# Attention output produced transposed: v as a 32-column stationary operand, sums from a tile of ones, inverted as exp(-ln)

## What is computed

```python
h = jnp.maximum(_layernorm(x, axis=-1), 0.0)
...
qkv = (x @ w_qkv).reshape(b, n, 3, H, hd).transpose(2, 0, 3, 1, 4)
q, k, v = (qkv[0], qkv[1], qkv[2])
attn = jnp.einsum('bhnd,bhmd->bhnm', q, k) * scale
attn = jnp.where(attn_mask[None, None] == 0, -jnp.inf, attn)
attn = jax.nn.softmax(attn, axis=-1)
o = jnp.einsum('bhnm,bhmd->bhnd', attn, v).transpose(0, 2, 1, 3).reshape(b, n, d)
o = o @ w_proj + b_proj
mu = jnp.mean(o, axis=-1, keepdims=True)
var = jnp.mean(jnp.square(o - mu), axis=-1, keepdims=True)
ln = (o - mu) * jax.lax.rsqrt(var + LN_EPS) * ln_gamma + ln_beta
return o + ln
```

## Time and profile before

| what | value |
|---|---|
| median of 3 runs | 1971.55 us (1969.12 to 1973.96) |
| span of the profiled execution, first to last instruction | 1971.0 us |
| busy: PE / PEld / DVE / ACT / POOL | 1831.1 / 1602.2 / 1609.3 / 1084.3 / 674.6 us |
| mean granted TensorE clock, share of the full one | 0.977 |

### The profile page before, as it was taken

The page is one execution under the profiler, slowest core; times in us unless marked ns, Lnnn a source line. Parts: engine busy times, 40 slices in busy tenths (PEclk is TensorE's granted clock), DMA queues, the critical chain, the costliest instruction groups (busy, mean ns, idle before and its releaser), DMA issues.

```text
span 1971.0 us, 39957 instructions
## 1 busy us (share of the span) xinstructions
PE 1831.1 (93%) x13064; PEld 1602.2 (81%) x13064; DVE 1609.3 (82%) x4485; ACT 1084.3 (55%) x2756; POOL 674.6 (34%) x1045
## 2 busy tenths in 40 slices
PE   6899999999999999999999999999999999999974
PEld 5788888878878888888878878788888878878864
DVE  3688897888888887887888888888887988978874
ACT  3555565655655555655655655655655655655632
POOL 3233333333333333333333333333332333333331
PEclk8999999999999999999999999999999999999987
DMA  2000000000000000000000000000000000000000
GB/s 88 12 17 17 23 23 11 21 16 16 21 17 16 22 16 17 21 16 16 22 16 16 21 17 16 22 16 16 22 16 16 22 16 16 21 16 17 12 6 17
DMA packets 37975, 37.85 MB, mean 19 GB/s; under 512 B 2416, under 2 KB 37488, under 8 KB 37872
## 3 DMA queue, kind: packets, MB, share of 16 engines
q1 hardware_dynamic: 37872, 36.84, 5.7%
HBM read 20.05 MB, written 16.78 MB: 19 GB/s over the span
## 4 chain that ended last, share of the span: by engine, by line
PE 48%; DVE 25%; issue 15%; POOL 9%; ACT 3%; DVEq 0%; POOLq 0%; DMA 0%; ACTq 0%
PE bank L314 15%; PE mid L387 11%; DVE stats L683 6%; DVE x L764 5%; PE bank L322 4%; POOL o_res L909 4%; POOL rstd L899 4%; PE bank L507 3%; PE mid L370 3%; PE bank L512 3%; PE bank L487 3%; DVE x L849 3%; DVE h_t_lo L699 2%; DVE o_gam L756 2%; ACT h_t_hi L559 2%
## 5 line engine op out<-in xcount | busy, mean ns | idle before, releaser
L567 ACT ACTIVATE probs<-mid,neg_max 128x128 f32<-128x128 f32 x1024 | 284.8, 379 | 105.2 <-DVE neg_max L713 105.2
L379 PE MATMUL mid<-k_diag,q_t 128*128 128x512 f32 x512 | 273.6, 617 | 0.0
L559 ACT ACTIVATE h_t_hi<-bank 128x512 fp32r<-128x512 f32 x192 | 114.9, 599 | 251.7 <-PE bank L322 251.6
L387 PEld LDWEIGHTS mid<-v,probs_t 128*128 128x128 f32 x2048 | 244.3, 192 | 3.3
L387 PE MATMUL mid<-v,probs_t 128*128 128x33 f32 x2048 | 239.9, 272 | 0.0
L899 POOL TENSOR_TENSOR rstd<-var_eps,minus_half 128x2 f32<-128x2 f32 x320 | 226.4, 707 | 25.1
L693 DVE TENSOR_SCALAR z<-x,mean_var,rstd 128x256 f32<-128x256 f32 x384 | 205.2, 575 | 10.8 <-POOL rstd L899 3.2
L713 DVE TENSOR_REDUCE neg_max<-mid 128x8 f32<-128x1024 f32 x128 | 154.6, 1208 | 51.1 <-issue 38.0
L897 POOL TENSOR_TENSOR var_eps<-mean_var,eps 128x2 f32<-128x2 f32 x320 | 66.0, 206 | 363.9 <-DVE mean_var L687 363.9
L322 PEld LDWEIGHTS bank<-ident,z 128*128 128x128 f32 x768 | 94.8, 152 | 112.4 <-DVE z L693 73.1
L322 PE MATMUL bank<-ident,z 128*128 128x128 f32 x768 | 125.8, 288 | 61.3 <-DVE z L693 61.3
(11 more groups left out here) (133 smaller groups left out, 5485.0 us busy)
## 6 DMA issues: line engine op xcount, KB each, us to landing
x<-in_x SPq DMA_DIRECT2D x64, 256.0 KB, 2.6
out_x<-x SPq DMA_DIRECT2D x64, 256.0 KB, 2.2
w_qkv_sb<-in_w_qkv SPq DMA_DIRECT2D x1, 768.0 KB, 4.8
w_q_sb<-in_w_q SPq DMA_DIRECT2D x1, 256.0 KB, 5.0
w_k_sb<-in_w_k SPq DMA_DIRECT2D x1, 256.0 KB, 5.3
w_proj_sb<-in_w_proj SPq DMA_DIRECT2D x1, 256.0 KB, 5.2
w_v_sb<-in_w_v_t SPq DMA_DIRECT2D x1, 256.0 KB, 5.4
w_gat_sb<-in_w_gat SPq DMA_DIRECT2D x1, 256.0 KB, 5.7
```

The source lines that it names most:

```text
L379: last = pe.matmul(mid[:, s], q_t[:, par, hc, b * N:(b + 1) * N], k_diag[:, hc, :, b * N:(b + 1) * N], start=False, stop=True)
L387: last = pe.matmul(mid[:, b, h * W33:(h + 1) * W33], probs_t[:, b * HC + h // RG, h % RG], v0[:, par, b, h], start=True, stop=True)
L559: act.activation(h_t[k][0][:], bank[:], ACT.Relu).then_inc(h_hi_ready[k], 1)
L567: last = act.activation(probs[:, s, r], mid[:, s, r * N:(r + 1) * N], ACT.Exp, bias=neg_max[:, s, r:r + 1])
```

## The change

The two operands of heads times values change places. `v0` of one head, 32 columns wide, is now the stationary operand, and `probs_t` moves, 128 columns. The result has 32 partitions (features) and 128 columns (nodes), so four heads are put beneath each other with `tile_position`, which places a 32-column operand at a column of the array and its result on the partitions of the same number. The outputs of both graphs fill bank 2 of `mid` and are transposed already. The sums come from a second product in the same form, with a 128x32 tile of ones as the stationary operand; they fill bank 0, repeated over the 32 partitions of their head. ACT takes the logarithm of the sums and then exp(-x) of that. DVE multiplies the two in one instruction (`o_norm`), ACT copies `o_norm` to `o_t_hi`, and DVE subtracts. The two calls of `divide_heads` and the four transposes of `o_heads` are gone. ACT's table set is named at the start; the built program loads a table once, as before.

The wait of the first block on `probs_t` moves from the second copy to the third, since bank 2 is written from the first block on, and `scores(0)` of the next step waits for the logarithm instead of `divide_heads`. `v0` loses its 33rd column.

```diff
@@ -93,7 +92,7 @@
         ident = sb("ident", [128, 128])
         ident_b = sb("ident_b", [128, 128], bf16)
         mask_b = sb("mask_b", [128, N], bf16)
-        ones = sb("ones", [128, 1])
+        ones = sb("ones", [128, HD])
         minus_half = sb("minus_half", [128, 2])
         eps = sb("eps", [128, 2])
         turn = sb("turn", [1, 1])
...
@@ -121,13 +120,14 @@
         q_t = sb("q_t", [128, 2, HC, 2 * N])
 
         k_diag = sb("k_diag", [128, HC, RG, 2 * N])
-        v0 = sb("v0", [128, 2, 2, H, W33])
+        v0 = sb("v0", [128, 2, 2, H, HD])
         BC = 2 * HC
         neg_max = sb("neg_max", [128, BC, RG])
         probs = sb("probs", [128, BC, RG, N])
         probs_t = sb("probs_t", [128, BC, RG, N])
-        inv_sum = sb("inv_sum", [128, 2, H])
-        o_heads = sb("o_heads", [128, 2, D])
+        ln_sum = sb("ln_sum", [128, 512])
+        inv_sum = sb("inv_sum", [128, 512])
+        o_norm = sb("o_norm", [128, 512])
         o_t = parts("o_t", [128, 2, C, N])
         o = sb("o", [128, 2, D])
         o_res = sb("o_res", [128, 2, D])
...
@@ -382,17 +382,25 @@
 
                 def heads_times_values(b):
 
-                    pe.wait_ge(probs_t_ready, done(p2, BC) - HC * (1 - b))
-                    for h in range(H):
-                        last = pe.matmul(mid[:, b, h * W33:(h + 1) * W33], probs_t[:, b * HC + h // RG, h % RG],
-                                         v0[:, par, b, h], start=True, stop=True)
-                    last.then_inc(heads_psum, 1)
+                    pe.wait_ge(probs_t_ready, done(p2, BC) - (1 - b))
+                    for s in (b * HC, b * HC + 1):
+                        to = slice(s * N, (s + 1) * N)
+                        for r in range(RG):
+                            at = slice(r * HD, (r + 1) * HD)
+                            pe.matmul(mid[at, 2, to], v0[:, par, b, (s - b * HC) * RG + r], probs_t[:, s, r],
+                                      start=True, stop=True, tile_position=(0, r * HD))
+                        for r in range(RG):
+                            at = slice(r * HD, (r + 1) * HD)
+                            last = pe.matmul(mid[at, 0, to], ones[:], probs_t[:, s, r],
+                                             start=True, stop=True, tile_position=(0, r * HD))
+                    if b == 1:
+                        last.then_inc(heads_psum, 1)
 
                 if middle:
                     pe.wait_ge(q_ready, done(p2))
                     pe.wait_ge(k_ready[0], done(p2))
                     pe.wait_ge(k_ready[1], done(p2))
-                    wait_before(pe, o_heads_ready, p2, 2)
+                    wait_before(pe, ln_sum_ready, p2)
                     scores(0)
                 if front:
                     pe.wait_ge(h_hi_ready[0], done(p1))
...
@@ -415,7 +423,7 @@
                     pe.wait_ge(q_ready, done(p1))
                     rows(bank6, h_t[0], w_qkv_p, 2 * D, v0_psum)
                 if middle:
-                    wait_before(pe, o_lo_ready, p2)
+                    wait_before(pe, o_norm_ready, p2)
                     wait_before(pe, o_ready, p2)
                     scores(1)
                 if gat:
...
@@ -526,19 +534,13 @@
                     elif on_before[0]:
                         wait_before(pe, h_lo_ready[0], p0)
                     transposes(bank7, z[0], 0)
-                if middle:
-                    for b in range(2):
-                        pe.wait_ge(o_heads_ready, done(p2, 2) - (1 - b))
-                        for c in range(C):
-                            last = pe.transpose(mid[:, 2, (b * C + c) * N:(b * C + c + 1) * N],
-                                                o_heads[:, b, c * 128:(c + 1) * 128], ident[:])
-                    last.then_inc(o_t_psum, 1)
 
             run(pe, step, {0: fold, 1: masks_and_fills, 2: other_weights})
 
 
         @block.scalar
         def _(act):
+            act.preload_act_table_set("natural_log_exp_and_others")
             act.wait_ge(w_qkv_in, 16)
             act.activation(w_qkv_p[0][:], w_qkv_sb[:], ACT.Copy).then_inc(w_hi_ready, 1)
 
...
@@ -570,7 +572,7 @@
 
                 def copy_probs_t(s):
                     act.wait_ge(probs_t_psum, done(p2, BC) - (BC - 1 - s))
-                    wait_before(act, heads_psum, p2, 2)
+                    wait_before(act, heads_psum, p2)
                     act.activation(probs_t[:, s], mid[:, s], ACT.Copy).then_inc(probs_t_ready, 1)
 
                 if front:
...
@@ -645,11 +647,19 @@
                     act.wait_ge(u_psum, done(p4))
                     wait_before(act, x2_exp_ready, p4)
                     act.activation(u_exp[:].rearrange("p b d -> p (b d)"), bank4[:], ACT.Exp).then_inc(u_exp_ready, 1)
+                if middle:
+                    act.wait_ge(heads_psum, done(p2))
+                    act.activation(ln_sum[:], mid[:, 0], ACT.Ln).then_inc(ln_sum_ready, 1)
+                    act.wait_ge(ln_sum_ready, done(p2))
+                    wait_before(act, o_norm_ready, p2)
+                    act.activation(inv_sum[:], ln_sum[:], ACT.Exp, scale=-1.0).then_inc(inv_sum_ready, 1)
                 if entry:
                     relu_hi(0, p0, bank7, [k_psum])
                 if middle:
-                    act.wait_ge(o_t_psum, done(p2))
-                    act.activation(o_t[0][:], mid[:, 2], ACT.Copy).then_inc(o_hi_ready, 1)
+                    act.wait_ge(o_norm_ready, done(p2))
+                    wait_before(act, o_psum, p2)
+                    act.activation(o_t[0][:].rearrange("p b c n -> p (b c n)"), o_norm[:], ACT.Copy)\
+                       .then_inc(o_hi_ready, 1)
 
             run(act, step, {1: copy_fold})
 
...
@@ -719,17 +729,6 @@
                         dve.tensor_tensor_reduce(out=s_prod[:, b, j], in0=hw[:, b], in1=a_gat_bc[:, j],
                                                  scale=1.0, scalar=0.0, op0=ALU.mult, op1=ALU.add,
                                                  accum_out=s_sb[:, b, j:j + 1]).then_inc(s_ready, 1)
-
-                def divide_heads(b):
-
-                    heads = mid[:, b, 0:H * W33].rearrange("p (h d) -> p h d", h=H)
-                    dve.wait_ge(heads_psum, done(p2, 2) - (1 - b))
-                    dve.reciprocal(inv_sum[:, b], heads[:, :, HD]).then_inc(inv_sum_ready, 1)
-                    dve.wait_ge(inv_sum_ready, done(p2, 2) - (1 - b))
-                    wait_before(dve, o_t_psum, p2)
-                    dve.tensor_tensor(o_heads[:, b].rearrange("p (h d) -> p h d", h=H), heads[:, :, 0:HD],
-                                      inv_sum[:, b].unsqueeze(2).to_broadcast([128, H, HD]), ALU.mult)\
-                       .then_inc(o_heads_ready, 1)
 
                 if middle:
                     maxima(0)
...
@@ -849,9 +844,14 @@
                         dve.scalar_tensor_tensor(x2[:, 1 - par, b], bank6[:, b * D:(b + 1) * D], inv_norm[:, b:b + 1],
                                                  x1[:, 1 - par, b], ALU.mult, ALU.add).then_inc(x2_ready, 1)
                 if middle:
+                    dve.wait_ge(heads_psum, done(p2))
+                    dve.wait_ge(inv_sum_ready, done(p2))
+                    wait_before(dve, o_lo_ready, p2)
+                    dve.tensor_tensor(o_norm[:], mid[:, 2], inv_sum[:], ALU.mult).then_inc(o_norm_ready, 1)
+                if middle:
                     dve.wait_ge(o_hi_ready, done(p2))
                     wait_before(dve, o_psum, p2)
-                    dve.tensor_tensor(o_t[1][:].rearrange("p b c n -> p (b c n)"), mid[:, 2],
+                    dve.tensor_tensor(o_t[1][:].rearrange("p b c n -> p (b c n)"), o_norm[:],
                                       o_t[0][:].rearrange("p b c n -> p (b c n)").bitcast(f32), ALU.subtract)\
                        .then_inc(o_lo_ready, 1)
                 if gat:
```

More of the change, by code:

```diff
@@ L44, in gnn_stack @@
     HC = H // RG
-    W33 = HD + 1
     SCALE = float(HD) ** -0.5
@@ L187, in gnn_stack @@
         probs_ready, probs_t_psum, probs_t_ready = sem("probs_ready"), sem("probs_t_psum"), sem("probs_t_ready")
-        heads_psum, inv_sum_ready, o_heads_ready = sem("heads_psum"), sem("inv_sum_ready"), sem("o_heads_ready")
-        o_t_psum, o_hi_ready, o_lo_ready = sem("o_t_psum"), sem("o_hi_ready"), sem("o_lo_ready")
+        heads_psum, ln_sum_ready, inv_sum_ready = sem("heads_psum"), sem("ln_sum_ready"), sem("inv_sum_ready")
+        o_norm_ready, o_hi_ready, o_lo_ready = sem("o_norm_ready"), sem("o_hi_ready"), sem("o_lo_ready")
         o_psum, o_ready = sem("o_psum"), sem("o_ready")
@@ L353, in masks_and_fills @@
             def masks_and_fills():
-                pe.wait_ge(fills_made, 5)
+                pe.wait_ge(fills_made, 4)
                 pe.wait_ge(mask_made, 1)
@@ L518, in step @@
                     for b in range(2):
-                        last = pe.matmul(bank5[:, 256 + b:257 + b], rel_sq[:, b], ones[:], start=True, stop=True)
```

(10 more changed lines are left out.)

## The result

The changed kernel takes 2031.01 us (median of 4 runs, 2026.17 to 2032.69), the kernel before 1971.87 in the same comparison: a ratio of 1.0293, 95% interval 1.0278 to 1.0308.

The account below looks back on a forecast made before the run. A step was taken as a PE half followed by a DVE half. 1.60 for DVE's half, 2 x 0.18 for the blocks and 0.32 for tiling changes gave 2.28 us per step, 146 over 64 steps: 2117 us, range 2040 to 2340.

Parts of the forecast that it names:

- What bounds it: Main loop step of 28.87 us: a PE half, then a DVE half; time on each engine counts in its own half alone.
- DVE's round trip: DVE half, `o_norm` to ACT's `o_t_hi` to `o_t_lo`: DVE stands still, 1.36 us per step, with no idle time to absorb it.
- Logarithm and exponential ahead of `h_t_hi`: ACT, behind the second block: they delay the ACTIVATE of L559 on the chain, +0.24 us per step, counted in DVE's half.
- The signs: Expected in the trace: block about 1.9 us, DVE idle about 0.7 before `o_t_lo`, L559's successor 0.5 behind the exponential, step about 31.2.
- the pace of the tiled passes: PE's blocks of head products: 32 passes run two overlapping, 1.89 us a block, +0.18 each; chance 0.55.
- The cost of changing the array's tiling: PE, four changes between whole and tiled array per step: 0.08 each, 0.32 per step, bounds 0 and 0.66.
- The first block: PE's first block of head products: +0.18 at two overlapping; four abreast gives back only 0.53, since PE then needs `att_norm`.
- the four-abreast rival: PE's blocks run four passes at once, -0.82 and -0.53 us: 0.57 per step, 2007 us; chance 0.13.
- The sum: Per step 1.60 + 2 x 0.18 + 0.32 = 2.28 us; over 64 steps 146, giving 2117 us.
- The range: Total time from 2040, between four and two abreast, to 2340, the serial case with its bound; holds 0.8.
- Hidden costs: Behind `o_t_lo` and `o_t_hi`: PE's output projection, late, stays hidden with 1.3 us to spare; `q_t` on ACT hidden too.

Follow-up runs that it names:

- e2: Changed kernel with DVE's multiplication `o_norm` moved ahead of `h_t_lo`; 1968.51 us, ratio 0.9982 to the kernel before.
- e4: Changed kernel with DVE's moments of stream 3 moved between `o_norm` and `o_t_lo`; 1987.09 us, ratio 1.0082 to the kernel before.
- e3: Changed kernel with ACT's logarithm and exponential moved behind `h_t_hi`; 2020.70 us, ratio 1.0246 to the kernel before.
- e1: Changed kernel with a block's products reordered, all four of one column position before the next position's; 2162.73 us, ratio 1.0968 to the kernel before.
- e9: Changed kernel with a block's products grouped by two column positions, heads 0 and 1, then 2 and 3; 2034.85 us, ratio 1.0320 to the kernel before.
- e6: Changed kernel with PE's main loop at two steps a turn in place of four; 2037.01 us, ratio 1.0322 to the kernel before.
- e5: e2 with PE's main loop at two steps a turn in place of four; 1950.19 us, ratio 0.9884 to the kernel before.
- e8: Changed kernel with the sums inverted by a reciprocal on DVE, not by exp(-ln) on ACT; 2253.44 us, ratio 1.1420 to the kernel before.

## Why the prediction was wrong

- **What bounds it** was right: a step is a PE half and a DVE half, and each part of the change counted only in its own.
- **DVE's round trip**, forecast at 1.36 us per step, measured 1.37 from `o_norm` to `o_t_lo`, and 1.35 in the length of the half. e2 and e4 take it away and get 1.23 and 0.79 back. Shown.
- **Logarithm and exponential ahead of `h_t_hi`**, forecast at 0.24, gave 0.16 in e3. Right in kind, a little too large. My place for its effect was DVE's half; it falls in PE's, which ends at `h_t_hi`. The signs came as written: DVE idle for 0.70 before `o_t_lo`, and `h_t_hi` 0.53 behind the exponential.
- **The step that failed** is the pace of the tiled passes: "each product's two passes go to the same one" (column tile), so two at a time, 1.89 us per block. It is 1.01, with all four side by side. I had reasoned that the second pass of a product holds up everything written behind it. e1 and e9 show that it does not. For the second block this makes -0.70 in place of +0.18.
- **The cost of changing the array's tiling**, 0.08 a change from a row of another kind, measured 0.10 and 0.09.
- **The first block** would by the four-abreast rival give back 0.53, the distance from its end to the end of `att_norm`. From PE's transposes of `z` (1001.19) to those of `att_norm` (1009.61) it is 8.42 us, 8.72 before: 0.30 back, as PE waits there for `att`, `att_norm`. But this is not PE's last wait. Right behind `att_norm` stands DVE's `rel`, for PE's products `bank<-v,rel`. Before, and in the changed kernel:

```profile
1072.18 0.42 DVE L826 TENSOR_TENSOR rel<-bank,adj_sb 128x256 f32<-128x256 f32 x1
1072.75 1.10 PE L507 MATMUL bank<-v,rel 128*128 128x256 f32 x4
```

```profile
1010.15 1.10 PE L515 MATMUL bank<-v,rel 128*128 128x256 f32 x4
```

`rel` ended at 1072.60 before and at 1010.00 after the change (the row of L825 above), and PE's products start 0.15 us behind it in both. Their other wait, for ACT's `v`, ended earlier, at 1071.92 and at 1009.33. From the transposes of `z` to these products it is 1072.75 - 1063.78 = 8.97 us before and 1010.15 - 1001.19 = 8.96 now. So PE came just in time before, and the first block had nothing to give: DVE's row through `att_norm` and `rel` holds PE to the same start at any faster pace. e1 bears this out from the other side: there the block is longer, `rel` ends at 1014.06 and its products start only at 1015.06, 0.27 behind the transposes. From the transposes of `att_norm` to the second block it is now 2.44, 2.05 before; of these 0.39, 0.29 is the wait for `rel` and 0.10 the change of tiling. No run took the wait for `rel` away. My prediction read only the wait for `att_norm`.
- **The sum** of PE's half: -0.30 + 0.39 - 0.70, and +0.19 behind the block (logarithm and exponential), gives -0.42. With +1.35 that is 0.93 per step. The forecast was 2.28, 1.35 too much: 0.94 of it is the second block with its two changes of tiling (-0.60 for +0.34), 0.35 the first block with its own (-0.01 for +0.34), 0.06 the round trip and the logarithm. The four-abreast rival, 2007 us, had the right pace and was 24 us too low, by the 0.36 per step that the wait for `rel` took from the first block. I gave it 0.13.
- **The range** began at 2040, between the two cases, and so left the measured one out.
- **Hidden costs**: the output projection and `q_t` were hidden, as forecast. Not thought of was that PE's longer code is fetched again at each turn. It cost next to nothing here (e6), but took 18 us of what e2 could have gained (e5).

## What to carry to other kernels

In this kernel float32 products on 32-column tiles ran four abreast although each has two passes (a block of 32 passes in 1.01 us), if the four positions came close behind one another. What this gives has then to be looked for on the chain: follow every wait up to the next block, not only the first, since here the second one (`rel`) took back all of the first block's 0.30. A product that delivers its output in another layout moves work between engines: a value that goes from DVE to ACT and back to the very next instruction cost both latencies in full (1.37 us), and moving it ahead of independent work (1.23 back per step in e2) was worth more than the 0.42 by which PE's half got shorter. When an engine's loop body grows, look at what its instruction queue moves.

## What the runs showed of the hardware that was not expected

- A busy column position did not block PE: by the two orders of e1 and e9, some four passes for it were put aside and the next position started (e1: 2.39 us for a block; e9: 1.03; changed: 1.01). The Trainium skill ("TensorE: Matmul & The Clock Gate", Part 3: Packing small matmuls) has matmuls start strictly in program order. No run here settles whether that holds. The traces record the eight passes of four products as within 0.43 - 0.27 = 0.16 us of one another, which is one pitch and not four: whether the array or the compiled program put the second passes behind the four first ones, the trace does not say.
- PE's loop body of the changed kernel was fetched again at every turn (148 KB on the mean), that of the kernel before was not (0.33 MB in all); with two steps a turn neither was (e5 and e6 0.29 MB). PE waited 2.9 us for it on the mean (40.6 us in 14 times), and behind a wait of 3.81 us the granted clock was 0.50 for the next 3.3 us (e2).
- A reciprocal on DVE took 3.35 us for 512 elements (e8).
